# Cross-attention over 16 sequences on one core: a rebuilt prologue, inputs prepared one by one, and an unrolled loop

## The reference, cut to what matters

```python
N, C, S, H = 16, 64, 256, 8                      # x, context: (16, 64, 256)
xn  = (x - mu) * rsqrt(var + 1e-5) * gamma + beta # mu, var over a whole sequence
q   = Wq @ xn + bq;   k, v = split(Wkv @ context + bkv)
att = softmax((q * 64**-.25).T @ (k * 64**-.25))  # per sequence and head, 256 x 256
y   = att @ v
out = x + Wo.T @ y + bo
```

## Time and profile before

| | us |
|---|---|
| three runs | 245.01, 246.27, 246.59 (median 246.27) |
| the profiled execution | 246.8, with a span of 245.0 |
| busy in the span | PE 214.4, DVE 214.4, POOL 195.6, ACT 194.2 |
| first score product (S of sequence 0) | at 43.87 |

### The profile page before, as it was taken

How to read it: one execution, slowest core, us unless ns; L and a number is a source line. 1 busy time by engine, 2 the same in 40 slices (tenths; PEclk the granted TensorE clock), 3 DMA queues, 4 the chain that set the end, 5 groups by cost and what they waited for, 6 DMA issues and landing times.

```text
span 245.0 us, 8138 instructions
## 1 busy us (share of the span) xinstructions
PE 214.4 (87%) x2746; PEld 199.0 (81%) x2746; DVE 214.4 (87%) x447; ACT 194.2 (79%) x391; POOL 195.6 (80%) x188
## 2 busy tenths in 40 slices
PE   0663597799889999999999999999999999998962
PEld 0563476699779999999999999999999999996851
DVE  3288998999997999999999999999999999997684
ACT  2244324999788999999999999999999999999860
POOL 3036995877998998989898989898989999998580
PEclk9999999999999999999999999999999999999996
DMA  6999601121032121212121212121212121010000
GB/s 141 219 284 211 141 3 55 32 58 36 2 89 64 36 68 35 64 33 64 33 64 33 64 33 64 33 64 33 64 33 64 37 64 36 13 33 17 13 0 23
DMA packets 13412, 15.08 MB, mean 62 GB/s; under 512 B 2064, under 2 KB 11920, under 8 KB 13200
## 3 DMA queue, kind: packets, MB, share of 16 engines
q1 hardware_dynamic: 13072, 14.16, 21.9%
q10 hardware_dynamic: 320, 0.66, 1.2%
HBM read 5.90 MB, written 1.05 MB: 28 GB/s over the span
## 4 chain that ended last, share of the span: by engine, by line
PE 64%; DVE 11%; POOL 9%; issue 5%; DMA 4%; ACT 4%; SPq 1%; POOLq 0%
PE ps_max L420 10%; PE ps_sc L401 10%; PE ps_sc L402 10%; POOL p_lo L609 8%; PE ps_t L383 6%; PE ps_z L361 6%; PE ps_z L363 5%; PE ps_z L362 5%; PE ps_t L384 5%; DMA x_res<-x_tiles 4%; PE ps_m L455 3%; PE ps_m L454 3%; DVE neg_max L738 1%; DVE x_seq L648 1%; ACT p_full L529 1%
## 5 line engine op out<-in xcount | busy, mean ns | idle before, releaser
L609 POOL TENSOR_TENSOR p_lo<-p_full,p_hi 128x512 f16<-128x512 f32 x122 | 142.8, 1189 | 23.1 <-ACT p_full L529 23.0
L738 DVE TENSOR_REDUCE neg_max<-ps_max 128x2 f32<-128x512 f32 x128 | 84.4, 663 | 0.0
L529 ACT ACTIVATE p_full<-ps_sc 128x512 f32<-128x512 f32 x128 | 78.4, 613 | 0.5 <-POOL p_lo L609 0.5
L527 ACT ACTIVATE p_hi<-ps_sc 128x512 f16<-128x512 f32 x128 | 77.0, 602 | 1.9 <-PE ps_sc L402 1.8
L401 PE MATMUL ps_sc<-t_a,c_seq 128*128 128x256 f32 x256 | 67.8, 286 | 0.2 <-ACT p_full L529 0.2
L402 PE MATMUL ps_sc<-t_b,c_seq 65*128 65x256 f32 x256 | 67.4, 284 | 0.0
L361 PEld LDWEIGHTS ps_z<-u_hi,p_hi 128*128 128x128 f16 x512 | 46.4, 97 | 13.2 <-issue 10.8
L361 PE MATMUL ps_z<-u_hi,p_hi 128*128 128x65 f16 x512 | 52.9, 194 | 3.2 <-DVE p_lo L783 2.4
L362 PE MATMUL ps_z<-u_lo,p_hi 128*128 128x64 f16 x512 | 52.7, 192 | 0.0
L363 PE MATMUL ps_z<-u_hi,p_lo 128*128 128x65 f16 x512 | 52.7, 193 | 0.0
L519 ACT ACTIVATE t_a<-ps_t 128x512 fp32r<-128x512 f32 x60 | 35.9, 598 | 18.5 <-PE ps_t L384 17.5
(11 more groups left out here) (101 smaller groups left out, 311.3 us busy)
## 6 DMA issues: line engine op xcount, KB each, us to landing
ctx_raw<-ctx SPq DMA_DIRECT2D x8, 256.0 KB, 17.0
c_seq<-c_all SPq DMA_DIRECT2D x16, 128.0 KB, 2.0
x_seq<-x_all SPq DMA_DIRECT2D x14, 128.0 KB, 2.0
c_max<-c_all SPq DMA_DIRECT2D x14, 128.0 KB, 2.0
x_res<-x_tiles SPq DMA_DIRECT2D x4, 256.0 KB, 7.2
z_n<-ctx_flat SPq DMA_DIRECT2D x1, 1024.0 KB, 14.7
c_seq<-c_all SPq DMA_DIRECT2D x16, 64.0 KB, 2.0
out<-x_res SPq DMA_DIRECT2D x16, 64.0 KB, 1.7
```

The source lines that it names most:

```text
L527: nc.scalar.activation(p_hi[:, buf, :, :].rearrange("p t s -> p (t s)"), scores, ACT.Exp).then_inc(act_phi, 1)
L529: nc.scalar.activation(p_full[:, head % 2, :], scores, ACT.Exp).then_inc(act_p, 1)
L609: nc.gpsimd.tensor_tensor(p_lo[:, buf, :, :].rearrange("p t s -> p (t s)"), p_full[:, head % 2, :], p_hi[:, buf, :, :].rearrange("p t s -> ...
L738: nc.vector.tensor_reduce(neg_max[:, (par + dn) % 2, head, :], ps_max[:, head % 2, :].rearrange("p (t s) -> p t s", t=KT), X, ALU.max, neg ...
```

## The change

- SP's loads in a new order (wk first; x and the context in smaller pieces; the large part of w on SP's queue), and ACT's queue carries only wq and two small pieces.
- The context is rounded by ACT (`c_high`, five pieces); the rest is taken by DVE for piece 0 and by POOL for the others (`c_low`; the last at step (2, 0)).
- The chain to `xn_scale` has one operation less; `a_low(1)` stands behind it, and sequences 0 to 3 are normalised by POOL. `x_high` now scales and rounds straight from `x_raw` on ACT.
- From sequence 6 on each sequence is prepared inside the steps, five sequences ahead: ACT at (m-5, 2), POOL at (m-5, 4), DVE at (m-4, 3).
- The 64 products for B stand between the first T and M, the bound and the scale of B later; B is scaled by ACT at (0, 0) and split by DVE at (0, 1); the first two U at (0, 2) and (0, 3), the next at (0, 6) and (0, 7).
- The bias is added to `x_res` in four pieces, at (1, 6), (5, 6), (9, 6), (13, 6). The loop is written out.

```diff
-        b_sb = p_full[:, 0, :]
+        b_sb = sb("b_sb", [P, H * C], fp32)[:]
...
+        X_HIGH_AT = {(-2, 3): 2, (-2, 5): 3, (-1, 2): 4, (-1, 4): 5} | {(m - 5, 2): m for m in range(6, N)}
+        X_LOW_AT = {(-1, 1): 2, (-1, 3): 3} | {(m - 4, 3): m for m in range(4, N)}
+        XN_AT = {(m - 5, 4): m for m in range(6, N)}
+        C_HIGH_AT = {(-2, 4): 1, (-1, 1): 2, (-1, 3): 3, (0, 3): 4}
+        XB_AT = {(c * CHUNK + 1, 6): c for c in range(N // CHUNK)}
+        C_LOW_AT = {(2, 0): 4}
...
-            with eng.Fori(FIRST // 2, (LAST + 1) // 2) as pair:
...
-            if isinstance(n, int) and (n, h) in ((-1, 7), (0, 1)):
-                return 0, -n, n + 1
+            if n == 0:
+                return {2: (0, 0, 0), 3: (0, 0, 1), 6: (1, 1, 0), 7: (1, 1, 1)}.get(h)
...
+            sp.dma_start(wk_sb, wk_in).then_inc(dma_qk, 16)
             for c in range(N // CHUNK):
                 sp.dma_start(x_res[:, chunk(c), :], x_tiles_in[:, chunk(c), :]).then_inc(dma_xt[c], 16)
-            sp.dma_start(x_raw[:, chunk(0), :], x_in[:, chunk(0), :]).then_inc(dma_x[0], 16)
+            load_x(sp, 0)
             load_ctx(sp, 0)
+            load_x(sp, 1)
+            sp.dma_start(w_sb[0:C, 0:W_BO], w_in[:, 0:W_BO]).then_inc(dma_w, 16)
+            load_ctx(sp, 1)
             sp.dma_start(ctx_spread, ctx_flat_in).then_inc(dma_flat, 16)
...
                     if m == 0:
                         if kt == 0:
                             pe.wait_ge(act_bhi, 1)
                             pe.wait_ge(dve_blo, 1)
...
                         else:
                             pe.wait_ge(dve_ulo, 1)
...
+            def x_high(m):
+                act.wait_ge(dma_x[next(g for g, (_, end) in enumerate(X_LOADS) if m < end)], 16)
+                for to in (x_seq[0:C, m, 0, :], x_seq[0:C, m, 1, :]) if m < DIRECT else (x_all[0:C, m, :],):
+                    last = nc.scalar.activation(to, x_raw[:, m, :], ACT.Identity, bias=xn_shift[0:C, m:m + 1], scale=xn_scale[0:C, m:m + 1])
...
+                if (m := XN_AT.get((n, h))):
+                    normalise(m)
+                if (c := C_LOW_AT.get((n, h))):
+                    pool.wait_ge(pool_plo, n * H + h)
+                    c_low(c)
+                if (c := XB_AT.get((n, h))) is not None:
                     pool.wait_ge(dve_bo, 1)
-                    nc.gpsimd.tensor_scalar(x_res[:], x_res[:], 1.0, bo2[:], ALU.mult, ALU.add).then_inc(pool_xb, 1)
+                    nc.gpsimd.tensor_scalar(x_res[:, chunk(c), :], x_res[:, chunk(c), :], 1.0, bo2[:], ALU.mult, ALU.add).then_inc(pool_xb, 1)
...
-            chain(nc.vector.tensor_scalar(y2[:], y1[:], -0.5, 1.5, ALU.mult, ALU.add))
-            chain(nc.vector.tensor_tensor(rstd[:], y0[:], y2[:], ALU.mult))
+            chain(nc.vector.scalar_tensor_tensor(out=y2[:], in0=y1[:], scalar=-3.0, in1=y0[:], op0=ALU.add, op1=ALU.mult))
...
+                if peeled_step(n, h, -1, 4):
+                    dve.wait_ge(dma_flat, 16)
+                    nc.vector.tensor_reduce(tops[:, 0:1], ctx_spread, X, ALU.max, apply_absolute_value=True).then_inc(dve_tops, 1)
```

More of the change, by code:

```diff
@@ L35 @@
 CHUNK = 4
-PIECES = ((0, 1), (1, 2)) + tuple((n, n + 2) for n in range(2, N, 2))
+C_PIECES = ((0, 2), (2, 4), (4, 8), (8, 12), (12, 16))
+X_LOADS = ((0, 2), (2, 4), (4, 16))
 U_TOP = 16384.0
@@ L176, in direct, with c_ready @@
             return isinstance(m, int) and m < DIRECT
[L178 to L184, removed]
+        def c_ready(eng, m):
+            piece = next(p for p, (_, end) in enumerate(C_PIECES) if m < end)
+            if piece:
+                eng.wait_ge(pool_clo, piece)
+            else:
+                eng.wait_ge(dve_clo, 1)
         def last_sequence(m):
@@ L204, in t_bank, with run @@
             return (ps_t[:], ps_z[:, 0], ps_z[:, 1])[turn % 3 if t_banks(turn) == 3 else 0]
[L207 to L216, removed]
-            with eng.Fori(FIRST // 2, (LAST + 1) // 2) as pair:
[L218 to L221, removed]
+        X_HIGH_AT = {(-2, 3): 2, (-2, 5): 3, (-1, 2): 4, (-1, 4): 5} | {(m - 5, 2): m for m in range(6, N)}
[4 more added lines that the diff above has]
+        C_LOW_AT = {(2, 0): 4}
+        def run(step):
+            for n in range(-3, N + 2):
                 for h in range(H):
@@ L295, in step @@
                                  rows_from[:, q, :]).then_inc(dma_negmax[q], 16)
-            run(sp, step)
+            run(step)
             for b in range(2):
@@ L418, in step @@
                     need(pe, dve_max, m * H + head - 1)
+                    if m == 0 and head < 2:
+                        pe.wait_ge(dve_alo, 2 * (head + 1))
+                        pe.wait_ge(act_ahi, 3 * (head + 1))
                     for qt in range(KT):
@@ L596, in _, with normalise @@
-            split_ctx(3)
-            def step(n, half, par, h):
-                if peeled_step(n, h, 1, 6):
+            xn_done = [0]
+            def normalise(m):
+                xn_done[0] = m + 1
+                pool.wait_ge(dma_x[next(g for g, (_, end) in enumerate(X_LOADS) if m < end)], 16)
+                nc.gpsimd.tensor_scalar(xn[:, m, :], x_raw[:, m, :], xn_scale[0:C, m:m + 1], xn_shift[0:C, m:m + 1],
+                                        ALU.mult, ALU.add).then_inc(pool_xn, 1)
@@ new lines, in c_low @@
+            def c_low(c):
+                first, end = C_PIECES[c]
+                pool.wait_ge(act_chi, c + 1)
+                pool.wait_ge(pool_xn, xn_done[0])
+                nc.gpsimd.tensor_tensor(c_all[C:P, first:end, :], ctx_raw[C:P, first:end, :], c_all[C:P, first:end, :].bitcast(fp32),
+                                        ALU.subtract).then_inc(pool_clo, 1)
+                pool.wait_ge(pool_clo, c)
+            pool.wait_ge(dve_scale, 1)
+            for m in range(4):
+                normalise(m)
@@ L636, in chain, with x_low @@
                 dve.wait_ge(dve_step, steps[0])
[L638 to L648 removed]
+            def x_low(m):
+                dve.wait_ge(act_xhi, m + 1)
+                dve.wait_ge(pool_xn, m + 1)
+                to = x_seq[:, m, 0, :] if m < DIRECT else x_all[:, m, :]
+                nc.vector.tensor_tensor(to[C:P], xn[:, m, :], to[0:C].bitcast(fp32), ALU.subtract).then_inc(dve_xlo, 1)
             def a_low(bank):
@@ L674, in _ @@
                                            op1=ALU.add).then_inc(dve_q, 1)
-            a_low(1)
+            dve.wait_ge(act_chi, 1)
+            first, end = C_PIECES[0]
+            nc.vector.tensor_tensor(c_all[C:P, first:end, :], ctx_raw[C:P, first:end, :], c_all[C:P, first:end, :].bitcast(fp32),
+                                    ALU.subtract).then_inc(dve_clo, 1)
             dve.wait_ge(pe_var, 1)
```

216 lines of the change are left out of this document (97 added, 119 removed).

## The result

The kernel after takes 264.13 us (median of 4 runs, 263.74 to 265.37), beside 246.29 for the kernel before on the same chip: ratio 1.072, 95% interval 1.067 to 1.078. The forecast was 252.7, with a range up to 256.5. The side was right, the size was not: 17.3 us more span (262.3 against 245.0) instead of 6.5.

The account below looks back on a forecast made before the run. PE was taken to set the pace, with POOL's list a second bound just under it. Terms -0.5 + 5.2 + 1.5 + 0.2 + 0.1 = +6.5 gave 252.7 us against 246.27, range 249.5 to 256.5.

Parts of the forecast that it names:

- POOL's 0.55 behind z: Steps of sequences 1 to 10: the added normalisation delays `p_lo`, costing 0.35 per sequence after 0.2 of slack.
- Up to the first T: Prologue: earlier loads and a shorter chain save 4.6 us, putting PE's first T product at 18.9.
- First S at 40.25: Prologue from first T: DVE paces, two `x_low` take 0.7, first S at 40.25 instead of 43.87.
- Sequence 0: First S to first `p_lo` of sequence 1: PE stalls of 1.2, 1.45 and 0.95 leave 0.5 of 3.6 gained.
- Sequences 1 to 10: Steady part: normalisation and `x_low` delay POOL's `p_lo`, 0.57 per sequence, nine times, 5.2 us in all.
- ACT's rounding at nothing: Steady steps: ACT's rounding of about 0.4 per sequence costs nothing, or 0.3 if its cover is gone.
- `x_low` by itself, 0.22: Steady steps at h = 3: DVE's `x_low` beside POOL's `p_lo` and z costs POOL 0.22 per sequence.
- Bias, 1.5 for three pieces: Sequences 5, 9 and 13: each bias piece stands ahead of `p_lo` of heads 6 and 7, costing 0.5.
- Loop at nothing: Whole loop: writing it out costs nothing, at most 0.5 gained.
- rival 1: Whole kernel: the head start is kept and everything added hides, PE alone the bound; 242.7 us, chance 0.14.
- rival 2: Whole kernel: half of each, sequence 0 covered, `x_low` free for POOL, bias 0.4 each; 247.0 us, chance 0.17.
- Rival 3: Sequence 0: stalls bring PE's lower clock level back for some 4 us of work, 2.2 lost; 254.9 us, chance 0.09.

Follow-up runs that it names:

- run 9: Kernel after with the prologue's `x_low` of sequences 2 and 3 (and the rounding of 3) moved to steps (-2, 3) and (-2, 4): 260.43 us (1.052).
- run 2: Kernel after with POOL's normalisation at h = 1 instead of h = 4 from sequence 6 on: 264.76 us (1.073).
- run 6: Kernel after with only POOL's normalisations of sequences 6 to 15 moved ahead of sequence 0, ACT's roundings staying at h = 2: 262.55 us (1.065).
- run 3: Kernel after with `x_low` computing only 8 of 256 columns from sequence 4 on: 264.65 us (one run).
- run 1: Kernel after with `x_low` at h = 7 instead of h = 3 from sequence 4 on: 277.5 us (1.127).
- run 5: Kernel after with only ACT's roundings of sequences 6 to 15 moved ahead of sequence 0, POOL's normalisations staying at h = 4: 275.76 us (1.110).
- run 8: Kernel after with `x_low` at h = 1 instead of h = 3, rounding and normalisation staying in the steps: 277.59 us (1.123).
- run 7: Kernel after with ACT's roundings ahead of sequence 0 and POOL's normalisation at h = 1 instead of h = 4: 256.09 us (1.040).
- v2b: Kernel after with roundings and normalisations of sequences 4 to 15 before sequence 0, B and U as before, `x_low` of 4 to 15 in the steps: 246.25 us (0.997).
- v2: As v2b, with `x_low` of sequences 8 to 15 made by POOL before sequence 0: 248.38 us (1.006).
- run 11: Kernel after with the bias pieces at h = 2 instead of h = 6: 262.06 us (1.058).
- v3: Kernel after with all preparation but four `x_low` ahead of sequence 0, B and U as before, bias at h = 2: 244.25 us (0.988), repeated 242.77 (0.986).

## Why the prediction was right or wrong

The sum was +6.5; the profiled execution shows +17.3. Term by term: up to the first `p_lo` of sequence 1, -0.5 forecast and +3.7 seen (62.97 against 59.26); around sequences 1 and 2, +0.2 and +0.8; from sequence 2 to 14, 6.8 (5.2, 1.5 and 0.1) and 12.0; the tail, 0 and 0.7. That the side was right is partly luck: the term that carried it, POOL's 0.55 behind z, measured nothing.

- **Up to the first T: right.** 18.9 forecast, 18.27 seen (16.5 to 19.3 in the other traces, with the same lists up to there); the operation that had taken 1.86 takes 0.18.
- **First S at 40.25: wrong, 43.35.** The step that failed is "two `x_low` 0.7 by estimate": they took 3.49, beside context pieces whose exclusion I had just read in the 1.86 of the same prologue. That is 2.8 of the 3.1. PE waited 3.67 for `tops`, which stands behind them on DVE. Run 9 gets 3.7 back at the first S.
- **Sequence 0: its mechanism right, a little small.** The handovers named are there: PE waits 0.78, 1.42 and 1.10 where 1.2, 1.45 and 0.95 were forecast. The first `p_lo` of sequence 1 came 19.6 after the first S, for which 18.5 was forecast.
- **Sequences 1 to 10: +5.2 forecast, 11.2 in nine intervals.** The cause was mistaken. The step that failed is "What waits is `p_lo` of heads 4 and 5, for it AV", and with it the price of 0.35 for POOL's 0.55: runs 2 and 6 take the 0.55 away and gain nothing per interval, POOL waits for ACT 15.8 us in the stretch, and PE waits for `p_lo` once. In its place the runs show PE waiting 1.1 per sequence for `t_b`, behind an `x_low` that lasts 1.52 instead of 0.4. "From above 0.85, if DVE holds POOL" looked at the exclusion from one side only: it was POOL that held DVE. The earlier trace rows showed z and then `p_lo` just at the time of h = 3, so the question "who has begun first?" could have been asked. The rule named from the Trainium skill ("SBUF — State Buffer", "Who interferes with whom") is borne out for one instruction, `x_low` ending with z in run 3, and the page also says that the order of issue decides who blocks; by that half of the rule, which I left out, the waiting one was DVE. That DVE waits through several instructions (runs 1, 5, 8) the rule as I told it didn't say.
- **ACT's rounding at nothing: wrong.** The forecast's reason was a cover, `p_full` of head 3 ready before POOL has done head 2. It failed: POOL waits 0.26 or 0.27 for it (the forecast's price for that case was 0.3). And `u_hi` had no cover at all. It is the first link of the chain: `x_low` asks 0.03 too late. Without the rounding (run 5) the second link appears, so it has no price of its own; with the normalisation at h = 1 it is worth 8 us (run 7 against run 2, by the ratios).
- **`x_low` by itself, 0.22: right.** Short and all else away, the interval is 12.34 (v2b), without it 12.08 (v2).
- **Bias, 1.5 for three pieces: somewhat high.** 0.33, 0.33 and 0.41 by the marks of run 11.
- **Loop at nothing: in line with the marks.** Written-out intervals of v3 are 12.05 to 12.10 where no bias stands, the loop's were 12.11. The unrolling wasn't tried alone.
- **Rivals 1 and 2** let what was added hide, whole or half. POOL's 0.55 did hide, as rival 1 had it; the total of neither came, since neither had a wait of DVE in it.
- **Rival 3, PE's clock:** in the steady part it isn't the cause, the granted clock is 1.00 there. Ahead of it, it has a share: matmuls of one form, which take 0.41 in run 9 where the granted clock reads 0.50, go from 0.41 to 0.28 at 46.55, 3.2 after the first S, where before the change they did so at 43.36, ahead of it. By an estimate from these rows (one every 0.21 against one every 0.12 for those 3.2 us) it is some 1.4 of the 3.7 up to the first `p_lo` of sequence 1, part of which the forecast had in "the lower pace of the first two S". The stalls in sequence 0, to which the rival tied it, didn't bring the lower level back in this trace; in run 9 it stands right behind them.

What stays open: why DVE gets in when it does. When, the traces show. Take every z_2 and every `x_low` of the steps, in all 19 traces, that asked while POOL worked and had its next instruction right behind. Asking within 0.05 of the start of POOL's instruction, it got in at once (62 times, all beside `p_lo`) or at the end of that instruction (69, all beside z); 0.10 into a bias piece it got in at once (7). Asking 0.32 to 0.63 into it, it stayed out until POOL stopped to wait for it, 33 times of 33 (all z_2, in runs 1, 3, 5 and 8). Asking 0.71 or later, it got in at the end of that instruction, 165 times of 168; the other three took 1.88, 2.53 and 4.13. The 0.7 at the tail wasn't looked into; the tail takes 20.3 to 21.2 in the other traces, whatever the edit, so it may not be the change's.

## What to carry to other kernels

An added instruction has three prices: its length, what it pushes back on its own engine, and what it then falls together with. For each vector instruction with two SBUF inputs, look up what GpSimd is doing at the moment at which it is asked for, and put it at a place where GpSimd pauses, or out of the loop. A busy share can't show this: DVE looked as loaded as before while it waited (126.45 against 126.11). The mean duration of one shape against its usual one does, and so does the table of PE's waits. Where a stage is paced by PE, move preparation into the gaps ahead of it, and check each gap's length and when its inputs land.
